# A layer norm's offset and scaled rows moved to ScalarE behind k2 and v2, and GpSimd's step reordered

## The reference, cut to what matters

```python
def _L0_attn_ref(x, Wq, bq, Wk, bk, Wv, bv, gamma, beta):
    ...
    kv = jnp.einsum('bnhd,bnhp->bhdp', k, v)
    ...
    out = (ctx / denom).reshape(B, N, C)
    y = out + x
    mu = y.mean(axis=-1, keepdims=True)
    var = y.var(axis=-1, keepdims=True)
    return (y - mu) / jnp.sqrt(var + EPS_LN) * gamma + beta

x = x + _L0_attn_ref(_L0_cond_ref(x, cond_1024, ...), ...)
x = x + _L0_ffn_ref(_L0_cond2_ref(x, cond_1024, ...), ...)
```

## Time and profile before

| what | us |
|---|---|
| median of 3 runs | 967.97 (966.38 to 970.36) |
| the profiled execution, its own time | 968.21 |
| its span in the profile | 966.5 |
| PE busy | 777.3 |
| DVE busy | 764.1 |
| POOL busy | 430.2 |
| ACT busy | 410.2 |

### The profile page before, as it was taken

How to read it: one execution, slowest core, us unless ns; L and a number is a source line. 1 busy time by engine, 2 the same in 40 slices (tenths; PEclk the granted TensorE clock), 3 DMA queues, 4 the chain that set the end, 5 groups by cost and what they waited for, 6 DMA issues and landing times. The chain is left out here.

```text
span 966.5 us, 22997 instructions
## 1 busy us (share of the span) xinstructions
PE 777.3 (80%) x7494; PEld 476.9 (49%) x7494; DVE 764.1 (79%) x1805; ACT 410.2 (42%) x1081; POOL 430.2 (45%) x596
## 2 busy tenths in 40 slices
PE   3447667788877878888876789999999999999965
PEld 1124344455545545555543446555555555555533
DVE  6177878777788787777764589999999999999983
ACT  2054545455555565555543333333333333333320
POOL 0055766766676666666652023233323323233332
PEclk9558879789899899888899989999999999999997
DMA  5864545556666666566531013332322333332232
GB/s 118 190 161 93 108 91 111 108 126 129 127 131 132 126 130 134 127 131 124 117 78 33 6 39 67 61 66 60 64 63 58 67 58 66 64 65 62 63 66 65
DMA packets 262382, 89.04 MB, mean 92 GB/s; under 512 B 233265, under 2 KB 261297, under 8 KB 262324
## 3 DMA queue, kind: packets, MB, share of 16 engines
q1 hardware_dynamic: 262324, 88.25, 44.5%
HBM read 25.19 MB, written 8.47 MB: 35 GB/s over the span
## 5 line engine op out<-in xcount | busy, mean ns | idle before, releaser
L782 PE MATMUL bank<-gu,xqT 128*128 128x512 f16 (+1 forms) x576 | 127.4, 368 | 8.0 <-DMA xqT<-xq_split 8.0
L728 POOL TENSOR_TENSOR ffn_room<-prob,h_coarse 128x704 f16<-128x704 f32 x32 | 44.1, 1378 | 154.0 <-DVE prob L171 154.0
L919 PE MATMUL bank<-wx,x1T 128*64 128x512 f16 x768 | 97.9, 392 | 4.2 <-DMA x1T<-x_split 4.2
L930 PE MATMUL bank<-wh,h 128*64 128x512 f16 x768 | 94.4, 381 | 0.7 <-ACT h L1184 0.7
L782 PEld LDWEIGHTS bank<-gu,xqT 128*128 128x128 f16 x576 | 55.9, 102 | 67.8 <-issue 12.0
L650 POOL TENSOR_TENSOR prob<-prob,row_max 128x520 f32<-128x520 f32 x64 | 68.8, 1075 | 42.3 <-DVE row_max L1349 42.3
L919 PEld LDWEIGHTS bank<-wx,x1T 128*64 128x64 f16 x768 | 78.7, 202 | 14.9 <-DMA x1T<-x_split 4.7
L1008 PE MATMUL bank<-dn,hqT 128*128 128x256 f16 x576 | 69.9, 277 | 7.6 <-DMA hqT<-ffn_room 6.6
L657 POOL TENSOR_TENSOR p<-prob,p 128x512 f16<-128x512 f32 x64 | 71.7, 1120 | 6.4 <-ACT p L1087 4.9
L810 PE MATMUL bank<-attn,xT 128*64 128x256 f16 x768 | 70.9, 337 | 0.0
L1008 PEld LDWEIGHTS bank<-dn,hqT 128*128 128x128 f16 x576 | 54.7, 99 | 26.5 <-issue 18.3
(11 more groups left out here) (192 smaller groups left out, 1888.1 us busy)
## 6 DMA issues: line engine op xcount, KB each, us to landing
vimg_in<-image_values SPq DMA_DIRECT2D x32, 136.0 KB, 3.1
x_in<-in_x_columns SPq DMA_DIRECT2D x16, 256.0 KB, 2.9
x_res<-in_x SPq DMA_DIRECT2D x16, 256.0 KB, 2.8
x_rows<-x_rows_sb SPq DMA_DIRECT2D x32, 128.0 KB, 1.8
ffn_room<-x_rows SPq DMA_DIRECT2D x64, 64.0 KB, 2.2
out<-ffn_room SPq DMA_DIRECT2D x64, 64.0 KB, 2.0
add_mask<-in_mask_Bx1x1xS_ff SPq DMA_DIRECT2D x2, 512.0 KB, 7.4
qkT<-qk SPq DMA_TRANSPOSE x64, 4.2
```

The costliest lines, as they stand in the source:

```text
L728: pool.tensor_tensor(blocks(hq_split[:, 0], FF), blocks(fp4_h.value, FF), spread(h_coarse, FF), ALU.mult).then_inc(s["hq_hi"], 1)
L782: last = pe.matmul(dst, lhs(a, c), rhs(b, c), start=first and c == 0 and a == b, stop=c == C - 1 and (a, b) == parts3[-1], skip_group_chec ...
L919: last = pe.matmul(bank[e][B * h:B * h + B, :], x1T16[m][:, c, :, at], half_cols(wx16, a, c, h), start=False, stop=True, skip_group_check= ...
L930: last = pe.matmul(bank[e][B * h:B * h + B, :], h16[:, m, c, :], half_cols(wh16, a, c, h), start=False, stop=True, skip_group_check=True)
```

## The change

ACT now makes `offset` itself, in two instructions of one number a partition: `neg_mean = -mean` (a copy with a scale) and `offset = neg_mean * rstd`. DVE's L1369 is gone. The two and z stand behind k2 and v2 in ACT's step, no longer at its head. In POOL's step the copy of the image keys, the image part of half 0 and the shift of half 1 stand ahead of the product with gamma and the sum. One wait is new on DVE: `bn_aggr` of a tile waits until `neg_mean` of the tile before is made.

```diff
@@ POOL, first stage, step
             if t2:
                 shift(t2, 0)
+            if t1:
+
+                after(pool, s["scores_ps"], t1.count(2, 2, back=1))
+                pool.tensor_copy(qkT[:, :, H // 2:H, S:KEYS].rearrange("p b g o -> p g (b o)"),
+                                 kimgT[:, :, bass.ds(t1.number() * 2, 2)]).then_inc(s["kimg_in"], 1)
+            if t2:
+                image_part(t2, 0)
+                shift(t2, 1)
             if t5:
 
                 pool.wait_ge(s["z_ready"], t5.count())
                 pool.tensor_tensor(zg_rows[:, :], z_rows[:, :], gamma_sb[:, :], ALU.mult).then_inc(s["zg_ready"], 1)
-            if t2:
-                image_part(t2, 0)
...
                 pool.tensor_tensor(x1_rows[:, t5.parity, :], zg_rows[:, :], xb_rows[:, :], ALU.add).then_inc(s["x1_ready"], 1)
-            if t1:
-
-                after(pool, s["scores_ps"], t1.count(2, 2, back=1))
-                pool.tensor_copy(qkT[:, :, H // 2:H, S:KEYS].rearrange("p b g o -> p g (b o)"),
-                                 kimgT[:, :, bass.ds(t1.number() * 2, 2)]).then_inc(s["kimg_in"], 1)
-            if t2:
-                shift(t2, 1)
+            if t2:
                 probs_lo(t2, 0)
@@ ACT, first stage, step
-            if t5:
-                act.wait_ge(s["offset_ready"], t5.count())
-                after(act, s["zg_ready"], t5.count(back=1))
-                act.activation(z_rows[:, :], res_rows[:, :], ACT.Identity, bias=offset[:, 0:1], scale=rstd[:, 0:1])\
-                    .then_inc(s["z_ready"], 1)
...
+            if t5:
+                act.wait_ge(s["mean_ready"], t5.count())
+                act.activation(neg_mean[:, :], mean_var[:, 0:1], ACT.Copy, scale=-1.0).then_inc(s["neg_ready"], 1)
+                act.wait_ge(s["neg_ready"], t5.count())
+                act.wait_ge(s["rstd_ready"], t5.count())
+                act.activation(offset[:, :], neg_mean[:, :], ACT.Copy, scale=rstd[:, 0:1]).then_inc(s["offset_ready"], 1)
+                act.wait_ge(s["offset_ready"], t5.count())
+                after(act, s["zg_ready"], t5.count(back=1))
+                act.activation(z_rows[:, :], res_rows[:, :], ACT.Identity, bias=offset[:, 0:1], scale=rstd[:, 0:1])\
+                    .then_inc(s["z_ready"], 1)
@@ DVE, first stage, step
-            if t5:
-                dve.wait_ge(s["rstd_ready"], t5.count())
-                after(dve, s["z_ready"], t5.count(back=1))
-                dve.scalar_tensor_tensor(out=offset[:, :], in0=mean_var[:, 0:1], scalar=-1.0, in1=rstd[:, :],
-                                         op0=ALU.mult, op1=ALU.mult).then_inc(s["offset_ready"], 1)
...
                 after(dve, s["var_ready"], t4.count(back=1))
+                after(dve, s["neg_ready"], t4.count(back=1))
```

More of the change, by code:

```diff
@@ L292, in program @@
     offset = sb("offset", [P, 1])
+    neg_mean = sb("neg_mean", [P, 1])
     z_rows = sb("z_rows", [P, D])
@@ L338, in program @@
         kv_ps kv_masked ctx_ps den_ready den_inv ctx_div resid stats_ready mean_ready var_ready
-        rstd_ready offset_ready z_ready zg_ready xb_ready x1_ready x1_hi x1_lo x1T_in
+        rstd_ready neg_ready offset_ready z_ready zg_ready xb_ready x1_ready x1_hi x1_lo x1T_in
         gates_ps sig_if sig_o tanh_g i_g cell_ready tanh_c h_ready h_hi h_lo
```

## The result

The changed kernel takes **954.73 us** (median of 4 runs, 953.43 to 955.28) against 969.16 of the kernel before in the same comparison (4 runs, 966.38 to 972.52): a ratio of 0.984 with an interval of 0.981 to 0.987. The profiled execution took 955.28, its span is 953.6. So the change gains 14 us where 33.5 were forecast. The LSTM's first product begins at 525.04 before and at 512.07 after, and 441.5 us follow it in both: the whole difference is in the first stage.

The account below looks back on a forecast made before the run. The prediction took a ring of waits through DVE's offset and ACT's z to bound the first stage. Gains of 27.5 (22 steps), 6 (early) and 0 (last) made 33.5 off 968.2: 935 us, range 914 to 957.

Parts of the forecast that it names:

- rival A: First stage: another ring, with PE's clock falls or late `pT` transposes, holds steps at 12.65: 953 us, chance 0.18.
- The ring of before: First stage, 13.35 us a step: DVE's offset delays ACT's z, then v2, PE's outer product and DVE's next maximum.
- The lock: DVE's L1369: 0.84 of its 1.00 us is exclusion by POOL's shift and does not follow the work to ACT.
- Rival C: ACT's small instructions cost 1.00 us each, so the z chain bounds: step 14.0, 982 us, chance 0.07.
- The two small instructions: ACT's `neg_mean` and `offset` behind v2: 0.20 us each, and 0.04 for each handover.
- The ring through POOL, 12.07: New first-stage step of 12.07 us, bound by `linear_kv`, v2, z, POOL, statistics, and back through PE.
- Queues behind: SP's `pT` transposes in time by 0.3 us, SP's order unchanged, `bn_aggr`'s new wait costing nothing, ACT's probabilities hidden.
- The term of the steady steps: 22 steps of the first stage, each going from 13.35 to 12.1 us: 27.5 us gained.
- The early steps: Six first-stage steps from 95.9 to 194.94 us: 1.0 us gained in each, 6 in all.
- The last steps: Steps behind 488.70 us and the single chain at the end: 0 gained, bounds -0.5 and +2.
- Wrong: DVE held at L1432 by the lower parts on POOL: Sign of a wrong forecast: DVE held there, so the statistics are late although `res_rows` is there; no size given.

Follow-up runs that it names:

- one_input_offset: The kernel before, with DVE's offset in the same place but its second operand a pointer scalar instead of a tensor: 941.34 us, ratio 0.971.
- late_store_after: The changed kernel, with SP's store of x1 moved behind the next step's transposes of q and k: 941.67 us, ratio 0.974.
- actq_after: The changed kernel, with the loads of the image values and of x sent through ACT's queue instead of SP's: 961.33 us, ratio 0.992.

## Why the prediction was half right

- *The time.* 954.73 lies within the range of 914 to 957, and that is luck: the range reaches so far only to take in rival A, whose mechanism is not what happened (below).
- *The ring of before* was read rightly. Taking the lock off it gave 1.21 us a step (13.33 to 12.12) in two independent ways, against 1.25 forecast. That the two numbers are so near is partly luck: the 1.25 was to come with z behind v2, while both of these kernels keep z at the head of ACT's step, and in one_input_offset the 1.21 are 0.79 of lock and about 0.4 of clock. Moving z was not needed.
- *The lock* ("0.84 of the 1.00"): 0.79 by one_input_offset. Rival C, the 1.00 as the work's own, is out.
- *The two small instructions*, 0.20 each: 0.20 and 0.30, with handovers of 0.03. The activation with a fixed scale costs 0.20, the one with a scale from memory 0.29 to 0.30, in all 32. The Trainium skill's 0.3 ("ScalarE: Activation LUTs", "Rules for kernel authors") is given for an activation with such an operand from memory (its bias), and fits the second; the prediction took it for both. The 0.1 more than forecast lies between its two bounds.
- *The ring through POOL, 12.07*: late_store_after runs at 12.20, the steps of actq_after without loads at 12.09. Right in size. In the changed kernel PE's waits for v2 are gone, POOL waits for z in 18 steps, 0.85 us each, and the statistics wait for `res_rows` in 13.
- *"Queues behind"* is **the step that failed**: "SP's order doesn't change", and only the landing of `pT` was counted. The order did not change, but its slack did. Behind the `pT` transposes SP works through the image values (1.50), x1T (1.23), the store (0.43), x (0.40) and gaps of 0.2 to 0.3 before it comes to q and k, 7.84 us from the first `pT`. This list did not become shorter, while the prediction's own sum put the split of q and k 2.14 us earlier and made the step 1.2 shorter, 3.3 together, against the 0.84 that SP had to spare; that is an estimate of 2.5 us late, and the trace shows 2.2 (a lag of 2.5 instead of 0.28). That SP waited for ACT's split 20 times in the 22 steps before (34.6 us in all) and for the same 8 times after (10.2 us) shows the slack being used up; it was in the trace before and was not read. The term of the steady steps was 27.5 and measured 8.6; late_store_after, which takes one issue out of this list, gives 25.3.
- *The clock*: rival A named the falls to 0.50 and steps that "settle at 12.65". Its time, 953, is nearest to the result, but its mechanism is not what happened: the steps do not settle at 12.65 but take turns, no engine waits for `pT` although it starts late in the long steps, and the clock is not a bound of its own here, since it is at 1.00 in 18 of 22 steps in late_store_after. In the change it fell right behind the 2.3 us in which PE waited for q and k, and the product behind that took 0.9 longer. Rival A was right that the clock carries much of the difference: of the 16.7 us between the 22 steps of these two kernels 10.0 are PE's busy time.
- *The early steps*: 6 forecast, 7.9 measured. *The last steps*: 0 forecast with -0.5 as the lower bound, -3.6 measured. The bound missed that z stands behind k2 and v2 there with nothing beside them: the shift of half 0 at 472.15 is followed by `res_rows` at 483.00, 10.85 later, and before by 8.50 (488.70 to 497.20). That is 2.35 of the 3.6. From there to the next `res_rows` it is 11.54 (to 494.54) against 10.48 before (to 507.68), 1.06 more, and the rest of the way differs by 0.2.
- *"Wrong: DVE held at L1432 by the lower parts on POOL"*: it was held, 1.34 us (now L1433, and as the median of all 32), where the median before was 0.57. It cost nothing in the step read, since DVE then waits another 1.24 for PE.

## What to carry to other kernels

An engine with nothing but DMA issues on it is in the ring too: when a change shortens a step, add up that engine's list of issues between the last thing it waits for and the first thing that someone waits for, and compare the slack with what the step is to lose. A small instruction that takes longer than its smallest copy may only be locked out by a neighbour, and another form of operand can be a cheaper cure than moving the work. Moves on two engines that make room for each other have to be priced together.

## What was not expected of the hardware

- The same arithmetic on 128 x 1 numbers takes 1.00 us with two tensors in the state buffer beside a running GpSimd instruction, and 0.21 with one tensor and a pointer scalar, in the same place.
- One DMA issue of 0.4 us more or less in SP's list moved the kernel up by 2.0% or down by 1.0%: it lengthens or shortens a wait of PE, and behind a wait of 2.3 us the product took 2.37 us at a granted clock of 0.50, instead of 1.46. In a kernel with about 0.8 us of slack on SP the same moved nothing.
- Three DMA issues from ScalarE's queue kept its own instructions away for 2.0 to 2.1 us, about what SP spends on them.
